# Reordered adds, a four-pass finite step and other normalise chunks in a fused graph-and-expert kernel

## The reference, cut to what matters

```python
x = x + gnn0(layernorm(x), adj)      # two layers, 128 -> 256 -> 128
x = x + experts(layernorm(x))        # 8 experts, top 1, 128 -> 512 -> 128, capacity 640 rows
x = x + adj @ (layernorm(x) * W)
x = x + routed_ffn(layernorm(x))     # per segment of 64 rows: shared + routed weights, 2 layers, 256 wide

# a layer of gnn0: column sums first, then the product
A = M / (sum(M, axis=0) + EPS);  W = where(A > THRESH, A, 0)
agg = W.T @ (h @ W_in + b_in) / (sum(W, axis=0) + EPS)
out = layernorm(agg @ W_out + b_out + h @ W_self + b_self) * gamma + beta

# the end of the experts
y = nan_to_num(y_tok, nan=0.0, posinf=10000.0, neginf=-10000.0)
```

## Time and profile before

| | |
|---|---|
| time before, median of 3 runs | 1105.76 us (1101.82 to 1106.72) |
| the profiled execution: time, span of its instructions | 1097.16 us, 1095.4 us |
| TensorE, VectorE, ScalarE, GpSimd busy | 92%, 53%, 30%, 21% of the span |
| mean granted TensorE clock | 0.967 of full speed |
| moved from and to memory | 220.96 MB, 203 GB/s over the span |

### The profile page before, as it was taken

The page is one execution under the profiler, slowest core; times in us unless marked ns, Lnnn a source line. Parts: engine busy times, 40 slices in busy tenths (PEclk is TensorE's granted clock), DMA queues, the critical chain, the costliest instruction groups (busy, mean ns, idle before and its releaser), DMA issues.

```text
span 1095.4 us, 12773 instructions
## 1 busy us (share of the span) xinstructions
PE 1011.4 (92%) x3570; PEld 532.9 (49%) x3570; DVE 575.3 (53%) x1564; ACT 327.5 (30%) x646; POOL 233.3 (21%) x232
## 2 busy tenths in 40 slices
PE   4889999999999999999997489948999999999997
PEld 2435545555455544444443268723454544454544
DVE  7777768877822224434433338853443434335265
ACT  4654663664421100000000045505123132232231
POOL 4011232242322112222222115543110100101101
PEclk9889999999999999999999589969999999999999
DMA  9969845555200388888780663325654654655400
GB/s 365 388 247 316 293 164 222 230 217 212 110 1 1 153 331 305 306 318 310 275 322 12 244 203 118 91 83 217 244 192 170 238 195 158 240 192 202 164 1 20
DMA packets 45356, 220.96 MB, mean 202 GB/s; under 512 B 6626, under 2 KB 27940, under 8 KB 33634
## 3 DMA queue, kind: packets, MB, share of 16 engines
q1 hardware_dynamic: 42146, 215.60, 52.9%
q0 software_dynamic: 2864, 4.39, 1.1%
q10 hardware_dynamic: 272, 0.13, 0.0%
HBM read 210.68 MB, written 11.62 MB: 203 GB/s over the span
## 4 chain that ended last, share of the span: by engine, by line
PE 71%; DVE 13%; ACT 4%; issue 4%; DMA 3%; DVEq 3%; ACTq 1%; POOL 1%; SPq 0%; POOLq 0%
PE PA L1488 29%; PE PA L1679 18%; DVE R L905 8%; PE O L1655 3%; ACT U L653 3%; PE O L1722 3%; PE O L1531 3%; DMA ring<-in_adj_cols 2%; PE PA L1451 2%; PE SR L1722 1%; PE SM L1722 1%; PE T L1742 1%; PE O L1701 1%; ACTq L705 1%; PE T L1731 1%
## 5 line engine op out<-in xcount | busy, mean ns | idle before, releaser
L1679 PE MATMUL PA<-ring,S 128*128 128x512 f32 x512 | 235.1, 599 | 3.4 <-ACT S L671 2.9
L1488 PE MATMUL PA<-ring,S 128*128 128x512 f32 x512 | 234.6, 608 | 2.0 <-DVEq L1007 2.0
L1488 PE MATMUL PA<-ring,U 128*128 128x512 f32 x512 | 225.5, 594 | 0.0
L1488 PEld LDWEIGHTS PA<-ring,S 128*128 128x128 f32 x512 | 97.6, 195 | 106.4 <-issue 105.3
L1488 PEld LDWEIGHTS PA<-ring,U 128*128 128x128 f32 x512 | 95.0, 190 | 107.3 <-issue 107.1
L1679 PEld LDWEIGHTS PA<-ring,S 128*128 128x128 f32 x512 | 92.9, 192 | 103.4 <-issue 98.4
L905 DVE TENSOR_TENSOR R<-R,ring 128x1024 f32<-128x1024 f32 x98 | 133.5, 1362 | 8.1 <-DMA ring<-in_adj_cols 1.7
L563 ACT ACTIVATE work<-ring 128x2048 int8<-128x2048 f32 x64 | 122.3, 1911 | 44.8 <-DMA ring<-in_adj_cols 41.4
L1357 DVE TENSOR_TENSOR U<-ring,work 128x512 f32<-128x512 f32 x112 | 82.6, 742 | 82.4 <-PE SR L1722 42.3
L813 POOL DMA_INDIRECT disp_d<-work x32 | 32.2, 1007 | 121.8 <-DVE work L1228 114.5
L845 POOL DMA_DIRECT2D out_x<-work x7 | 5.9, 844 | 233.4 <-DVE work L1428 233.4
(11 more groups left out here) (234 smaller groups left out, 1161.0 us busy)
## 6 DMA issues: line engine op xcount, KB each, us to landing
ring<-in_adj_cols SPq DMA_DIRECT2D x56, 2048.0 KB, 7.8
ring<-in_adjT_cols SPq DMA_DIRECT2D x32, 2048.0 KB, 7.2
ring<-in_Wr SPq DMA_DIRECT2D x1, 4096.0 KB, 13.0
ring<-in_Wr SPq DMA_DIRECT2D x2, 2048.0 KB, 13.7
work<-in_w SPq DMA_DIRECT2D x16, 256.0 KB, 3.6
disp_d<-U SPq DMA_DIRECT2D x4, 650.0 KB, 12.0
work<-disp_d SPq DMA_DIRECT2D x8, 325.0 KB, 3.2
S<-in_x SPq DMA_DIRECT2D x4, 512.0 KB, 5.7
```

Of the source, the lines that this page charges most:

```text
L1488: mm = nc.tensor.matmul(out_T[:, :], X[:, t * D:(t + 1) * D], ring[slot][t // HT][:, (t % HT) * BW:(t % HT + 1) * BW], start=n == 0, stop= ...
L1679: mm = nc.tensor.matmul(PA[slot][:, :], S[:, t * D:(t + 1) * D], ring[1][t // HT][:, (t % HT) * BW:(t % HT + 1) * BW], start=t == 0, stop= ...
```

## The change

Five things are edited. (1) In the first layer two of the four pieces of quarter 1 of block k+2 are added ahead of `layer2_inputs`. (2) `finite` becomes four passes: a mask of what is not finite times zero, a clamp to +-10000, a product with "is at most infinity", and a predicated copy of that onto `y` where the mask is set. For the last expert the PSUM read of the second part stands inside the finite step of the first. (3) The normalise chunks are 3, 3, 4, 6, 8, 8 tiles instead of 4, 4, 4, 6, 6, 8; VectorE normalises only the first, and takes the moments of the second before it does; minus the mean is made on VectorE, POOL multiplies it by the deviation's inverse, and ScalarE normalises in one pass. (4) In the last stage the third raw copy stands behind the last staged tile, the second one tile earlier; `turn_routed(1)` stands at tile 18 instead of 19 and `routed(2)` at tile 21 instead of 20. (5) ScalarE reads the expert number of a group's first segment before it waits for the group.

```diff
-CHUNKS = ((0, 4), (4, 8), (8, 12), (12, 18), (18, 24), (24, 32))
-FIRST = 2
+CHUNKS = ((0, 3), (3, 6), (6, 10), (10, 16), (16, 24), (24, 32))
+FIRST = 1
+RAW_AT = (5, 8, 15)
...
@@ ScalarE, normalise @@
                 if c >= FIRST:
                     act.wait_ge(s_rstd3, c + 1)
+                    alone(act)
                     for t in range(lo, hi):
-                        nc.scalar.activation(S[:, t * D:(t + 1) * D], R[:, t * D:(t + 1) * D], ACT.Identity, bias=nm3[:, t:t + 1])
-                    act.drain()
-                    for t in range(lo, hi):
-                        last = nc.scalar.activation(S[:, t * D:(t + 1) * D], S[:, t * D:(t + 1) * D], ACT.Copy, scale=rstd3[:, t:t + 1])
+                        last = nc.scalar.activation(S[:, t * D:(t + 1) * D], R[:, t * D:(t + 1) * D], ACT.Identity,
+                                                    bias=nm3[:, t:t + 1], scale=rstd3[:, t:t + 1])
...
@@ ScalarE, last stage @@
+                    e = act.value_load(route_sb[0:1, ds((k - 1) * SB + s, 1)], min_val=0, max_val=E2 - 1)
                     if s % SH == 0:
                         act.wait_ge(s_rt, (k - 1) * NG + n // SH + 1)
                         alone(act)
-                    e = act.value_load(route_sb[0:1, ds((k - 1) * SB + s, 1)], min_val=0, max_val=E2 - 1)
...
@@ GpSimd, normalise, behind ve3 and the power @@
+                    power.then_inc(s_pow3, 1)
+                    pool.wait_ge(s_pow3, c - FIRST + 1)
+                    alone(pool)
+                    nc.gpsimd.tensor_tensor(nm3[:, lo:hi], nm3[:, lo:hi], rstd3[:, lo:hi], ALU.mult).then_inc(s_rstd3, 1)
...
@@ VectorE, first layer, step(k) @@
                     scales(k + 1)
+                if k + 2 < NB:
+                    add_quarter(k + 2, 1, (0, 1))
                 if k > 0:
                     layer2_inputs(k - 1)
                 if k + 2 < NB:
-                    add_quarter(k + 2, 1)
+                    add_quarter(k + 2, 1, (2, 3))
...
@@ VectorE, experts, finite(n, between=None) @@
-                    nc.vector.tensor_scalar(fin, y, 0.0, 0.0, ALU.mult, ALU.is_equal)
-                    nc.vector.tensor_scalar(pos, y, FMAX, BIG, ALU.is_gt, ALU.mult)
-                    nc.vector.tensor_scalar(neg, y, -FMAX, -BIG, ALU.is_lt, ALU.mult)
+                    nc.vector.tensor_scalar(odd, y, 0.0, 0.0, ALU.mult, ALU.not_equal)
+                    nc.vector.tensor_scalar(lim, y, BIG, -BIG, ALU.min, ALU.max)
                     dve.drain()
-                    nc.vector.tensor_scalar(y, y, FMAX, -FMAX, ALU.min, ALU.max)
+                    if between is not None:
+                        between()
+                    nc.vector.scalar_tensor_tensor(sub, y, INF, lim, ALU.is_le, ALU.mult)
                     dve.drain()
-                    nc.vector.tensor_tensor(y, y, fin, ALU.mult)
-                    dve.drain()
-                    nc.vector.tensor_tensor(y, y, pos, ALU.add)
-                    dve.drain()
-                    nc.vector.tensor_tensor(y, y, neg, ALU.add).then_inc(s_y, 1)
+                    nc.vector.copy_predicated(y, odd, sub).then_inc(s_y, 1)
...
-                read(1).then_inc(s_ye, 1)
-                finite(0)
+                if e < E1 - 1:
+                    read(1).then_inc(s_ye, 1)
+                    finite(0)
+                else:
+                    finite(0, lambda: read(1))
...
@@ VectorE, normalise @@
+            def moments_y(c):
+                lo, hi = CHUNKS[c]
+                add_y(c)
+                dve.drain()
+                for t in range(lo, hi):
+                    nc.vector.bn_stats(st6[:, 6 * (t - lo):6 * (t - lo) + 6], R[:, t * D:(t + 1) * D])
+                dve.drain()
+                for t in range(lo, hi):
+                    last = nc.vector.bn_aggr(mv3[:, 2 * t:2 * t + 2], st6[:, 6 * (t - lo):6 * (t - lo) + 6])
+                if c >= FIRST:
+                    dve.drain()
+                    last = nc.vector.tensor_scalar(nm3[:, lo:hi], tiles(mv3, NT, 2)[:, lo:hi, 0], -1.0, None, ALU.mult)
+                last.then_inc(s_mv3, 1)
+                dve.drain()
+
+            moments_y(0)
+            for c in range(1, len(CHUNKS)):
+                moments_y(c)
+                if c == FIRST:
+                    for first in range(FIRST):
+                        dve.wait_ge(s_rstd3, first + 1)
+                        alone(dve)
...
...
@@ VectorE, last stage @@
-                        if n >= 5 and n % SH == 1:
-                            raw_rows(k, n // SH - 1)
+                        if n in RAW_AT:
+                            raw_rows(k, RAW_AT.index(n))
...
@@ TensorE, last stage, TAIL3 @@
-                     (17, lambda k: turn_routed(k, 0)), (19, lambda k: turn_routed(k, 1)), (20, lambda k: routed(k, 2)),
+                     (17, lambda k: turn_routed(k, 0)), (18, lambda k: turn_routed(k, 1)), (21, lambda k: routed(k, 2)),
```

More of the change, by code:

```diff
@@ L178, in build @@
         e_y = [R[:, CAP * i:CAP * (i + 1)] for i in range(2)]
-        e_fin, e_pos, e_neg = [R[:, CAP * (2 + i):CAP * (3 + i)] for i in range(3)]
+        e_lim, e_sub = [R[:, CAP * (2 + i):CAP * (3 + i)] for i in range(2)]
+        e_odd = R[:, CAP * 4:CAP * 5].bitcast(I32)
         e_prob = [R[:, CAP * 5 + 8 * i:CAP * 5 + 8 * i + CT] for i in range(2)]
@@ L828, in _ @@
             for c, (lo, hi) in enumerate(CHUNKS):
-                if c >= FIRST:
-                    pool.wait_ge(s_mv3, c + 1)
-                    nc.gpsimd.tensor_scalar(nm3[:, lo:hi], tiles(mv3, NT, 2)[:, lo:hi, 0], -1.0, 0.0, ALU.mult, ALU.add)
-                inv_sqrt(hi - lo, tiles(mv3, NT, 2)[:, lo:hi, 1], s_mv3, c + 1, s_rstd3, c + 25 + XC, ve3[:, lo:hi], rstd3[:, lo:hi])
+                pool.wait_ge(s_mv3, c + 1)
+                alone(pool)
+                nc.gpsimd.tensor_scalar(ve3[:, lo:hi], tiles(mv3, NT, 2)[:, lo:hi, 1], LN_EPS, 0.0, ALU.add, ALU.add).then_inc(s_ve, 1)
+                pool.wait_ge(s_ve, c + 25 + XC)
+                alone(pool)
+                power = nc.gpsimd.tensor_tensor(rstd3[:, lo:hi], ve3[:, lo:hi], neg_half[:, 0:1].to_broadcast([P, hi - lo]), ALU.pow)
+                if c < FIRST:
+                    power.then_inc(s_rstd3, 1)
+                else:
+                    power.then_inc(s_pow3, 1)
+                    pool.wait_ge(s_pow3, c - FIRST + 1)
+                    alone(pool)
+                    nc.gpsimd.tensor_tensor(nm3[:, lo:hi], nm3[:, lo:hi], rstd3[:, lo:hi], ALU.mult).then_inc(s_rstd3, 1)
             def step3(k, slot, rnd, prev, nxt):
```

22 lines of the change are left out of this document (9 added, 13 removed).

## The result

The changed kernel took 1089.64 us (median of 4 runs, 1089.53 to 1091.95), the kernel before on the same chip 1104.71 us (4 runs, 1101.82 to 1106.72): 15 us less, a ratio of 0.9868 [0.9847, 0.9889]. The two profiled executions are closer: 1097.16 us before, 1089.61 after, 7.5 us apart. So the timed runs gained twice what the traces did. Before's timed runs lay 7.6 us over its profiled one, those of the changed kernel are level with theirs. Every other trace in this document is of one of its kernel's timed runs. Before's is not one of its four here, and on which chip it was taken is not on record.

What follows compares the result with a forecast made beforehand. TensorE, holding 71% of the chain, was taken as the bound, so gains come from its waits. 3.5 + 1.5 + 4.2 + 0.8 = 10.0 us off 1097.16, scaled by ratio to 1095.7 us; range 1090.8 to 1101.

Steps and rivals of the forecast that it cites:

- first layer: First layer: adding two pieces ahead of `layer2_inputs` lets `collect` start earlier and shortens `raw_sums` waits; 3.5 us, bounds 0 to 3.6.
- experts' end: Last expert: fewer finite passes and the second read between them start the first scatter earlier; 1.5 us taken.
- normalise: Normalise: new chunks split the 2.86 us wait into 0.4 and 0.9 and keep the clock full; 4.2 us, bounds 1.5 to 5.4.
- last stage: Last stage: moving group 2 removes 4.5 us of waits, new waits inside group 3 leave 0.8 us net; bounds -1 to 4.4.
- the forecast's ratio of 0.9909: Whole kernel: predicted time over before's timed median, carried from the profiled execution; 1105.76 x 0.9909 = 1095.7 us.
- the shared lock: First layer: VectorE and GpSimd share an SBUF port, so piece 1 waits for POOL's whole add and ends at 235.8.
- no wait over 0.1 us: First layer: expected sign that no wait over 0.1 us stands in front of `raw_sums` except the one of 1.78.
- the discount for a possible dear instruction: Last expert: 1.6 us gain falls to 0.5 if integer mask and predicated copy each cost a pass more; 1.5 taken.
- rival (b): Last stage: staged tiles are in time and all 4.5 us are gained; 13.7 us off, 1092 us; chance 0.18.
- the last step: Whole kernel: the profiled execution lies 0.8% under the timed median, so its ratio 0.9909 is carried over, giving 1095.7 us.
- For the first seven experts I count nothing: First seven experts: no gain, since outputs scatter during the next expert and VectorE waits for TensorE at the reads.

Runs made afterwards that it cites:

- e3: Changed kernel with the old seven-pass finite step and early second read in all experts: 1089.99 us, ratio to before 0.9943.
- e4: Changed kernel with all four pieces of the quarter added behind `layer2_inputs` again, as before: 1090.47 us, ratio to before 0.9946.
- e6: Changed kernel with the old seven passes in the first seven experts only: 1085.54 us, ratio to before 0.9914.
- e7: Changed kernel with the old seven passes and early second read in the last expert only: 1086.06 us, ratio to before 0.9919.
- e8: Changed kernel with group 3, group 2's transposition and the last transposition each one product tile later in the last stage: 1080.65 us, ratio to before 0.9869.
- e9: Changed kernel with the old order of the adds and six more small VectorE semaphore instructions in the first expert: ratio to before 0.9951.
- e11: Changed kernel with the normalise's chunks, two ScalarE passes and POOL's and VectorE's order of before: 1091.98 us, ratio to before 0.9971.
- e12: Changed kernel with the last stage's old places of group 2, second transposition, raw copies and expert-number load: 1086.78 us, ratio to before 0.9923.
- e2: The changed kernel repeated without an edit: 1084.88 us, ratio to before 0.9896.
- e1: The kernel before, repeated without an edit: 1095.24 us, ratio 0.9994.
- e5: The kernel before with the change's new finite step alone: 1096.46 us, ratio to before 1.0015.
- e13: The changed kernel without an edit, on another chip where before took 1107.96 us: 1090.40 us, ratio to before 0.9837.
- e15: The kernel before with one 1.25 us VectorE instruction more ahead of the first read in each expert: 1108.76 us, ratio to before 0.9999.
- e14: Changed kernel with 116 more small VectorE semaphore instructions, 14 or 15 in each expert: 1101.67 us, ratio to before 0.9941.

## Why the prediction was wrong, and where it was right

**The terms were near.** Measured over the traces: first layer 4.0 us (first to eighth `raw_sums` on average 263.3 us in the eight later traces with the old order, and 265.6 in the first one of before; 259.2 in eleven with the new) for 3.5; experts' end 1.9 for 1.5; normalise 3.6, between 2.5 and 4.8, for 4.2; last stage 0.7 for 0.8. The sum is 10.2 for 10.0, and on the second chip the timed runs gave 11.2 [9.0, 13.8]. That is the only run of the unedited changed kernel on a chip where before takes 1095 to 1096 us. An estimate from the eight edited ones there (e3, e4, e6 to e9, e11, e12), each less what its trace shows of its edit, puts the change at 0.989 to 0.9925, 9.6 us on average. So on these chips the forecast's ratio of 0.9909 stands. The 7.5 us between the first two traces hold the same terms: first layer 6.1 (with the 1.78 us of that one execution), normalise 3.2, experts' end 1.0, last stage 0.7, less 4.2 that the changed kernel lost between experts, and 0.7 in small differences.

**First layer, right, its reason thin.** `collect` did go to its product's end and the shared lock did price piece 1, but VectorE comes 1.1 us early, not 0.3: in the block shown piece 1 ends 4.5 us behind piece 0's start (4.7 in the prediction), the two pairs take 1.6 us with what idles ahead of them (1.7) and pieces 2 and 3 take 3.2 (3.5). The forecast that no wait over 0.1 us would remain was wrong: 0.27 us stay between `collect` and the fold.

**Experts' end, right within 0.4 where results are not late.** The integer mask took 0.36 us and the predicated copy 0.58, no dearer than a pass, so the discount for a possible dear instruction was not needed. In e2 the first scatter starts 8.11 us behind the product's start; before it was 9.58. The 1.9 us are e3's; e7 gives 1.3, and the first two traces 1.0.

**Normalise, right.** The waits were 0.73 or 1.33 us and 0.90, and the clock held. In the old order warm-up to tile 16 took 23.9 to 26.2 us in eight traces, in the new one 21.4 to 21.7 in twelve. Only the long wait is followed by the low clock, for a varying time or not at all: behind it the granted clock reads 0.50 from 744 to 750 us in e1, and 1.00 in e5, whose warm-up to tile 16 takes 23.9 us for e1's 26.2. So the term was never sharper than 1 us to either side.

**Last stage, right by number only.** The prediction took the difference between 0.77 and 0.47 us as given and credited it to the moved groups. It is ScalarE's pause, and the groups themselves give nothing. The 0.39 us inside group 3 were forecast at 0.5, but such a stop costs 0.60, not the 0.52 of the sum; that rival (b) is out is shown by the same row.

**What failed is the last step, "That execution lies 0.8% under the median of the timed runs, so I carry the ratio over".** The scaling itself changes nothing, for 1105.76 - 10.0 is 1095.8 too. What was wrong is what the step takes for granted: that the 8.6 us between before's profile and its timed runs (7.6 by the four runs) are time that the change leaves alone. They were not, for the changed kernel's runs on that chip have no such distance. Before's 1097.16 us fit the chips where it takes 1095 to 1096 us, so its rows probably show an execution without the losses of its timed runs. With this the step "For the first seven experts I count nothing" fails on such chips. On the first chip and e13's the seven distances between experts of the changed kernel take 4.2 and 5.1 us more than elsewhere and its last expert's end 1.0 and 1.2, about its 4.8 and 5.5 us over e2. Before was 8.7 and 11.9 us over the 1096.05 us that it took beside e2. The change saves the differences there, 3.9 and 6.4 us, beyond e2's 11.2. That is arithmetic on the same timed runs and names no stage.

**What stays open.** That before loses these 9 to 12 us in its experts is argued, not shown: no trace of it from such an execution exists, nor one of the changed kernel with seven passes. The strongest sign is e15, before with one instruction more in each expert, which on e13's chip ran as long as before. Outside the experts its trace keeps e1's pace: 263.1 us from first to eighth `raw_sums` (e1: 264.0), 26.1 from warm-up to tile 16 (26.2), 311.8 from there to the last product (311.8). All that it takes more lies in the seven distances, 11.9 us, and the last expert's end, 1.7. The code of the other stages is before's own, so before's 11.9 us are most likely in its experts too. Why seven passes would lose more there than four is less clear. e14 adds only 14 or 15 tiny VectorE instructions to each expert, where VectorE idles, and its distances are 7.4 us longer than e13's; the old finite step has ten instructions more than the new one in each expert. But in e14's experts the granted clock also reads 0.50 twice, for 3.4 us each time, and in e13's never, so a part of the 7.4 may be the clock's. Against a simple rule: e6, with seven passes in seven experts on another chip, shows nothing of the kind. Why TensorE's results arrive late there is not settled; in the first trace of the changed kernel, in e13 and in e15 it happens with the granted clock at 1.00 through all experts.

## What to carry to other kernels

Compare a profiled execution with the timed runs before summing against it; where they differ by as much as the change is worth, find the stage that differs before summing, for the change may touch it. See that the trace and the timed runs are of one chip. When one part of a change is undone, look whether the stages that it doesn't touch kept their pace; if not, pad the instruction count and measure again. A step moved behind its own wait should take the next consumer with it: group 2 alone gave nothing, groups 2 and 3 together 3.9 us.

## What the hardware showed

- VectorE and ScalarE pause 0.3 to 0.35 us behind every 128th instruction of their streams. The page's DMA part has two instruction queues, q14 with packets of 8,192 bytes and q8 with packets of 16,384. In the last stage of e14 a packet of q14 starts 0.7 us behind each of VectorE's pauses, at the places where its 116 more instructions had moved them. So the pause goes with the load of instructions; whether it is caused by the step from one packet to the next was not tested.
```profile
q8 instruction: 28, 0.46, 0.2%
q14 instruction: 46, 0.38, 0.1%
```
- A VectorE add with both inputs in SBUF that began 0.83 us into a 2.97 us POOL instruction took 3.23 us for 1.23; VectorE instructions with an input in PSUM took their 0.42. In the first traces of both kernels the slowed adds began 0.14 to 1.27 us into a POOL instruction, and each ended 1.08 or 1.09 us behind that instruction's end.
- A wait of 0.39 us in the middle of group 3's 16 products cost TensorE 0.60 us: 2.55 us from start to end for 1.95.
- On the first result's chip and on e13's the time from the experts' product to VectorE's second read was longer, 6.33 us for 4.97 in the expert shown, at a granted clock of 1.00; the kernel with seven passes took 9 to 12 us more there than elsewhere, the one with four 5.
